# Map stage: inverse roots by Newton steps on VectorE, and a new order of feed-forward, squares and windows

## The reference

```python
x = x + conv_block(ln_c(x))      # windowed attention, then the map part
t = tokens(x)
t = t + ffn(ln_t(t))             # values rounded to fp8 (5,2) and fp16
x = from_tokens(t)

# map part of conv_block, on the attention result x2 (+ biases dw_b, fc2_b):
y   = gelu((layernorm(x2) * n2w + n2b) @ fc1_w + fc1_b)  # 96 -> 192
dw  = gelu(depthwise_conv_5x5(y) + dw_b)
x2  = (y + dw) @ fc2_w + fc2_b + x2                      # 192 -> 96

# ffn: h = relu(qlinear(t, W1, b1)), 96 -> 384; y = qlinear(h, W2, b2)
```

## Time and profile before

| | us |
|---|---|
| median of 3 runs | 7757.35 (7748.72 to 7774.06) |
| profiled execution | 7760.73, span 7758.4 |
| map stage in the profile | from about 3921 to the end |

### The profile page before, as it was taken

One profiled execution on the slowest core, in us unless ns is written; L12 is line 12 of the kernel. 1 busy time (PEld: TensorE's weight loads), 2 busy tenths in 40 slices (PEclk: granted clock), 3 DMA queues, 4 the chain that ended last, 5 costly groups with the idle time before them and its releaser, 6 DMA issues.

```text
span 7758.4 us, 207703 instructions
## 1 busy us (share of the span) xinstructions
PE 7010.4 (90%) x75964; PEld 4335.4 (56%) x75964; DVE 5160.8 (67%) x7973; ACT 4781.1 (62%) x7962; POOL 2218.8 (29%) x2024
## 2 busy tenths in 40 slices
PE   8969999999999999999958988989898889989987
PEld 3325555545545555555546666666666666666664
DVE  6867777777777777777745556556555655555564
ACT  6636656656655656566526666666666666666665
POOL 0013433334333443334312222222222222222221
PEclk9979999999999999999969999999999999999998
DMA  7744344444444444444323333333333333333332
GB/s 210 229 133 98 93 97 102 102 94 96 99 98 97 101 98 98 92 103 101 81 62 79 80 76 70 78 79 69 74 82 76 68 78 80 71 74 79 77 68 46
DMA packets 444703, 715.58 MB, mean 92 GB/s; under 512 B 116426, under 2 KB 358940, under 8 KB 419264
## 3 DMA queue, kind: packets, MB, share of 16 engines
q1 hardware_dynamic: 444209, 708.90, 38.8%
HBM read 395.33 MB, written 166.64 MB: 72 GB/s over the span
## 4 chain that ended last, share of the span: by engine, by line
SPq 19%; PE 19%; issue 4%; DVE 4%; ACT 2%; DMA 2%; DVEq 0%; ACTq 0%; POOLq 0%; POOL 0%
SPq L1101 19%; PE P L1269 6%; PE P L1258 3%; PE P L1328 3%; PE P L1247 3%; DVE Z L1685 2%; PE P L1278 2%; DMA YS<-Y 2%; PE P L1237 1%; DVE H L1714 1%; DVE H L1709 1%; ACT Y L1499 1%; PE P L1315 1%; ACT P L1505 1%; PE P L1213 0%
## 5 line engine op out<-in xcount | busy, mean ns | idle before, releaser
L820 DVE TENSOR_REDUCE NM<-P 128x4 f32<-128x1024 f32 x1444 | 1764.2, 1222 | 592.7 <-PE P L654 588.5
L768 ACT ACTIVATE PROB<-P 128x1024 f32<-128x1024 f32 x1444 | 1399.9, 1021 | 1025.8 <-PE P L669 1025.8
L1328 PE MATMUL P<-FC,XN 97*126 97x192 f32 x5408 | 1000.4, 330 | 41.1 <-ACT Y L1499 40.2
L1163 POOL TENSOR_TENSOR T<-T,Y 96x512 f16 (+1 forms) x260 | 305.9, 1176 | 2516.6 <-DVE Y L1718 2516.6
L1328 PEld LDWEIGHTS P<-FC,XN 97*126 97x126 f32 x5408 | 885.4, 188 | 196.1 <-issue 140.7
L669 PE MATMUL P<-QF,KS 32*128 32x256 f32 x11552 | 833.8, 403 | 112.0 <-DVE QF L815 111.3
L1499 ACT ACTIVATE Y<-P 126x384 f32<-126x384 f32 x1352 | 750.7, 618 | 238.2 <-PE P L1328 222.7
L669 PEld LDWEIGHTS P<-QF,KS 32*128 32x128 f32 x11552 | 525.0, 185 | 635.7 <-DVE QF L815 574.3
L505 POOL TENSOR_TENSOR Y<-XHS,RNS 96x512 f32<-96x512 f32 x304 | 598.0, 1993 | 820.3 <-DMA RNS<-rnorm 515.0
L677 PE MATMUL P<-PROB,V 128*32 128x256 f32 x11552 | 778.3, 387 | 1.4 <-ACT PROB L768 1.4
L1247 PEld LDWEIGHTS P<-Y,WC 127*50 127x50 f32 x19968 | 577.9, 140 | 180.1 <-DVE Z L1685 112.9
(11 more groups left out here) (149 smaller groups left out, 11273.6 us busy)
## 6 DMA issues: line engine op xcount, KB each, us to landing
YS<-Y SPq DMA_DIRECT2D x2080, 48.8 KB
RBC<-sums SPq DMA_DIRECT2D x456, 160.0 KB, 3.2
X<-x2map SPq DMA_DIRECT2D x52, 1344.0 KB, 8.3
XHS<-xhat SPq DMA_DIRECT2D x76, 768.0 KB, 6.3
RNS<-rnorm SPq DMA_DIRECT2D x38, 1536.0 KB, 9.5
x2map<-XHS SPq DMA_DIRECT2D x76, 768.0 KB
T<-in_x SPq DMA_DIRECT2D x52, 960.0 KB
out<-T SPq DMA_DIRECT2D x52, 960.0 KB, 4.9
```

Source lines behind the costliest of these rows:

```text
L768: A.activation(PROB[:, par, u:u + 2, :], P[:, B_ST[u]:B_ST[u] + 2, :], ACT.Exp, scale=DQ ** -0.5).then_inc(act_exp, 1)
L820: V_.tensor_reduce(NM[:, :, :].rearrange("p a (u d) -> p u a d", d=32)[:, 2 * i:2 * i + 2, :, DQ], P[:, B_S[0]:B_S[0] + 2, :].rearrange("p ...
L1328: m = M.matmul(P[0:KW, WBANK[r], i * MLP:(i + 1) * MLP], xnf[:, RI * WX * w:RI * WX * w + KW], FC1[:, :], start=True, stop=True)
```

## The change

- The root on ACT and the reciprocal on DVE are replaced: `parts` now adds 1e-5 to the variance (read from PSUM), makes a first guess by integer shift and subtraction, and refines it by three Newton steps of three DVE instructions each. `std2` and `std3` are gone. The gathered variance of `gather2` moves from bank 2 to the second half of bank 7; turn 1, which writes that bank, waits until DVE has read it.
- hidden 0 to 2 and output 0 (with hidden16, out16, hidden8 in their order on ACT and DVE) now run in the body of their own strip, among the last windows. On the other end, output 4 goes behind conv 11, and the DVE steps out16 3 and 4 go directly ahead of parts2. POOL's `end` 0 to 2 run at the end of their own strip's body, 3 and 4 in the next one, after means 0 and 1.
- The squares have five buffers instead of two (three of them lie in Z). The first five squares of strip u + 2 run at the end of body u, where PE also does var2 0 and 1; the rest follows in the next body.
- `begin` is cut into five pieces that follow means 2 to 6.
- Windows use banks 4 to 6 only; all of the orders of PE, ACT and DVE are rewritten. The SP queue issues the same transfers, with the condition on `begin` as a count of five.

```diff
-WBANK = [4 + r % 3 for r in range(12)] + [(0, 1, 4, 5, 6)[(r - 12) % 5] for r in range(12, NG)]
+NEARLY = 3
+WBANK = [4 + r % 3 for r in range(NG)]
...
-        B_VAR2, B_REP2, B_VAR3 = 7, 2, 7
+        B_VAR2, B_REP2, B_VAR3 = 7, 7, 7
...
+        SQB = [SQ[:, 0, :], SQ[:, 1, :]] + [zf[:, i * FT:(i + 1) * FT] for i in range(3)]
...
                 n = times(pool, u, NX)
...
-                    for j in range(NF):
+                    for j in range(NEARLY, NF):
                         end(o0, t0, j)
+                nxt = u + 1 if isinstance(u, int) else pool.snap(u + 1)
                 for j in range(NSLOT, NX):
                     means(n, third, j, first)
-                if follow:
-                    begin(u + 1 if isinstance(u, int) else pool.snap(u + 1))
+                    if follow:
+                        begin(nxt, j - NSLOT)
+                for j in range(NEARLY):
+                    end(times(pool, u, NF), third, j)
...
-                small(V.reciprocal(RCP[:, :], STD[:, :]))
+                V.tensor_scalar(STD[:, :], rep, 1e-5, None, ALU.add).then_inc(read, 1)
+                dve.wait_ge(read, nth)
+                small(V.tensor_scalar(bits, STD[:, :].bitcast(int32), 1, None, ALU.logical_shift_right))
+                small(V.tensor_scalar(bits, bits, -1.0, 1597463007.0, ALU.mult, ALU.add))
+                for _ in range(3):
+                    small(V.tensor_tensor(res, RCP[:, :], RCP[:, :], ALU.mult))
+                    small(V.scalar_tensor_tensor(res, res, -0.5, STD[:, :], ALU.mult, ALU.mult))
+                    small(V.scalar_tensor_tensor(RCP[:, :], res, 1.5, RCP[:, :], ALU.add, ALU.mult))
                 small(V.tensor_copy(RB[:, :], RCP[:, :]))
```

More of the change, by code:

```diff
@@ L1152, in _, with begin @@
             G = nc.gpsimd
[L1154 to L1159, removed]
+            def begin(u, j):
+                if j == 0:
+                    pool.wait_ge(xo_loaded, u * 32 + 32 if isinstance(u, int) else pool.snap(u * 32 + 32))
+                    pool.wait_ge(x2_loaded, u * 16 + 16 if isinstance(u, int) else pool.snap(u * 16 + 16))
+                t = T[:, tch(slot_of(pool, u), j)]
+                G.tensor_tensor(t, t, X2[:, 2 * W + j * FT:2 * W + (j + 1) * FT], ALU.add).then_inc(pool_x, 1)
             def end(o0, third, j):
@@ L1249, in conv, with turn @@
                 m.then_inc(pe_conv, 1)
-            def turn(n7, n12, j):
+            def turn(v, n7, n12, j):
                 if j == 0:
                     hold(pe, pe_passed, dve_ys, n12 + NCG)
+                if j == 1 and v is not None:
+                    hold(pe, pe_passed, dve_read2, v + 1)
                 if j >= 2:
@@ L1398, in body @@
                 beside(spread2, v, v7, 5)
-                turn(n7, n12, 6)
+                turn(v if follow else None, n7, n12, 6)
                 beside(spread2, v, v7, 6)
@@ L1452, in _ @@
             windows(0, 0, *range(NG))
+            for j in range(2):
+                var2(NL, j)
             strips(pe, body)
@@ L1455, in _ @@
             for j in range(NF):
-                hidden(last, j)
-                output(last, j)
+                if j >= 3:
+                    hidden(last, j)
+                if j >= 1:
+                    output(last, j)
         @block.scalar
@@ L1516, in turned, with body @@
                 z.then_inc(act_z, 1)
-            def body(u, prev, follow):
+            def body(u, prev, follow, more):
                 v = u + 1 if isinstance(u, int) else act.snap(u + 1)
@@ L1560, in body @@
                 convolved(n12, 11)
-                beside(std2, v)
+                ffn(out16, 4)
                 turned(n7, 0)
@@ L1598, in body @@
                 beside(windows, v26, 23)
+                hidden16(n5, 1)
                 beside(windows, v26, 24)
                 beside(windows, v26, 25)
+                ahead(square2, w, w7, 2)
+                ahead(square2, w, w7, 3)
+                out16(n5, 0)
+                hidden16(n5, 2)
+                ahead(square2, w, w7, 4)
+                out16(n5, 1)
             for j in range(NL):
                 square2(0, 0, j)
-            std2(0)
             windows(0, *range(NG))
+            for j in range(5):
+                square2(1, NL, j)
             strips(act, body)
@@ L1608, in _ @@
             for j in range(NF):
-                hidden16(last, j)
-                out16(last, j)
+                if j >= 3:
+                    hidden16(last, j)
+                if j >= 2:
+                    out16(last, j)
         @block.vector
@@ L1745, in body @@
                 add_centres(u, n12, 2)
-                ffn(out16, 2)
+                ffn(hidden8, 4)
                 add_centres(u, n12, 3)
@@ L1749, in body @@
                 add_centres(u, n12, 5)
-                dve.wait_ge(pool_x, u + 1)
-                ffn(hidden8, 4)
+                beside(sum2, v7)
                 add_centres(u, n12, 6)
-                beside(sum2, v7)
                 add_centres(u, n12, 7)
@@ L1787, in body @@
                 scale3(n5, 4)
+                hidden8(n5, 0)
+                hidden8(n5, 1)
+                out16(n5, 0)
+                hidden8(n5, 2)
+                hidden8(n5, 3)
+                out16(n5, 1)
+                out16(n5, 2)
             sum2(0)
-            dve.wait_ge(act_std, 1)
-            parts(1, dve_parts2)
+            parts2(0, 1)
             for j in range(NL):
@@ L1796, in _ @@
             for j in range(NF):
-                hidden8(last, j)
-                out16(last, j)
+                if j >= 4:
+                    hidden8(last, j)
+                if j >= 3:
+                    out16(last, j)
 def constants():
```

212 lines of the change are left out of this document (101 added, 111 removed).

## The result

The changed kernel takes 8036.32 us (median of 4 runs, 8032.76 to 8043.06) against 7759.12 us for the kernel before in the same comparison (4 runs, 7748.72 to 7774.06). The ratio is 1.0356, 95% interval 1.0343 to 1.0369: slower by 277 us, where about 193 were forecast. The direction was right; the time lies 86 us above the forecast of 7950 and 21 us above the range's upper end of 8015.

The account below looks back on a forecast made before the run. A 71.08 us ring, gone round 51 times, bounds the kernel; 41.2 + 12.8 + 20.9 = 74.9 us, so 7757.35 + 195 - 1.3, about 7950 us. Range 7730 to 8015 us; forecast's own 7880 to 8000.

Parts of the forecast that it names:

- The ring: Map stage: 51 equal strip-to-strip steps of 71.08 us set the time; forecast to become 74.9 us each.
- Part A: First windows matmul to first addition of centres, 40 sync-queue issues: 41.8 us before, forecast 41.2, moved feed-forward steps covered.
- Part B: Conv phase, first addition of centres to first turn: 13.66 or 12.55 us before, forecast 12.8 with low clock.
- Part C, the roots without POOL: Turns and fc2: twelve new DVE instructions make the roots 5.1 us instead of 2.4, hidden, leaving 15.85 us.
- rival 3: New DVE instructions take 0.45 us each, or feed-forward steps outlast the centres' landing: above 8015 us; chance 0.08.
- Part C, the port: Turns and fc2: POOL instructions hold up DVE's small ones beside parts2; PE stalls 2.8 to 4.0 us, taken as 3.4.
- Part C, the clock: Turns and fc2: after PE's stall, 1.2 GHz for some 3.3 us of dense work, costing 1.65 us.
- Outside the ring: First strip's roots +2.2 us; at the end parts3 +2.3, overlapped hidden/output rounds -5.3, last conv phase -0.5: together -1.3.
- Rival 1: Port costs little: parts2 ends by 7.1 us, stall 0 to 0.85 us, 7690 to 7737 us; chance 0.18.
- Rival 2: Port stalls PE but the clock stays up: ring 72.7 to 73.9 us, 7835 to 7900 us; chance 0.15.
- Rival 4: Reordering leaves the ring unchanged: the 40 issues dominate, other terms cancel, 7735 to 7780 us; chance 0.07.

Follow-up runs that it names:

- the two runs with old roots: Changed kernel with ACT's square root and DVE's reciprocal put back for both norms, 7873.9 us; put back for norm 2 alone, 7685.98 us.
- the kernel with POOL quiet: Changed kernel with POOL waiting for parts2 before means 2, end 3, 4 and begin moved behind means 3: 7690.17 us.
- both filled kernels: Unused matmuls between turn 3 and spread2 0: four in the changed kernel, 7929.86 us; two in the one with the residual add behind all copies, 7772.36 us.
- the old order with Newton roots: Kernel before with only the roots changed to Newton for both norms, old order, banks and buffers kept: 7790.18 us, ratio 1.0034.

## Why the prediction was right in direction and short in size

**The ring.** Right. All of the map stage is 51 equal steps, and (76.79 - 71.08) x 51 = +291 us of the spans' difference, 8036.0 - 7758.4 = 278.

**Part A,** forecast 41.2, measured 40.96: right. The cover held; no instruction of the feed-forward network moved into it came onto the ring. The statement beside it, that ACT is not on the ring at the table loads, so that their loss gains nothing, is true of the old order only. In the new one, with three banks, the loads of norm 3's root would cost about (7874 - 7686) / 51 = 3.7 us a ring, by the two runs with old roots. Norm 3's Newton root was needed for the new order; I priced the parts of the change one by one and missed that two of them hold each other up.

**Part B,** forecast 12.8, measured 12.95: right, with the low clock before conv 3 as said. It is low for 3.4 us in one kind of strip and for 6.8 us in the other, and slows fewer chunks in the first.

**Part C, the roots without POOL,** forecast 5.1 us and no wait: measured 5.1 us, right to the tenth. The 0.45 us apiece of rival 3 is out.

**Part C, the port,** the mechanism as in the earlier trace rows: right, by the rows above and by the kernel with POOL quiet. The size fell short at one choice. parts2 was to end 9.1 us after the first turn, or 10.3 if the copies block too; it ended at 10.4, and the wait was 4.0 us, the upper bound. I had taken 3.4, the middle. Two copies block, 0.6 us each. The Trainium skill, "GPSIMD Engine Reference", section 8 (Key points), which excepts no GpSimd instruction, would have given the 4.0; the trace agrees with it here. Term: +0.6 us a ring, +31 us.

**Part C, the clock.** This step failed, in size: 1.65 us was forecast, with bounds of 1.2 and 2.1. Measured, 22.87 - 15.81 - 4.0 = 3.1 us are lost beyond the wait on average. The clock itself is 2.1 and 2.8 us of that in the two kinds of strip (22.50 and 23.23 against 20.40 with the wait filled), 2.5 on average. The rest is 0.6 us that I left out: spread2 stands 4.2 us later than in the quiet kernel and not 4.0, and 0.4 us stay in both filled kernels, whose cause was not tried. The clock was sized too low because from the earlier trace rows I took 3.3 us of dense work. That low stretch is 3.4 us long in all, and PE idles in its first 0.8 us. Here the stretch is 6.8 us, with 5.1 or 6.6 us of work in it. The trace of the kernel before has stretches of 6.8 us as well, but only four beside 73 of 3.4 in the map stage. What makes one long or short stays open. Term: 3.1 instead of 1.65, +1.4 us a ring, +74 us.

The two terms together: 0.6 + 1.4 = 2.0 us, against 76.79 - 74.9 = 1.9 measured. The port's term stayed within its bounds, the clock's did not, and the latter alone put the time outside the range: with 3.4 and 3.1 us the sum gives 8025 us, with 4.0 and 2.1 it gives 8004. There is a slip in the forecast's own range, too: its upper ring of 75.9 us leaves out the 0.4 us of doubt on A and B, and should be 76.35 (8025 us). Even so the measured 76.79 lies above it.

**Outside the ring,** forecast -1.3 us; the spans give 278 - 291 = -13. The time to the first landing is 5.1 us less (the earlier trace rows against 4036.99) where 2.2 more was forecast. But the kernels here that share this stage have it anywhere from 4024 to 4041, so I don't read a cause from it. After the last landing it is 82.9 us instead of 91.1, 8.2 less where 3.5 was forecast. Which of its three terms is larger wasn't tried.

**The rivals.** Rival 1, the port costing little, at 7690 to 7737 us: ruled out for the changed kernel, but it is what the kernel becomes when POOL is kept away (7690, the range's lower end). Its point of decision, parts2 ending by 7.5 us after the turn, was placed rightly: the kernels of the new order with 4.0, 5.3 and 5.9 us are faster, those with 8.3 and 10.4 slower. (With both old roots it is 4.0 and the kernel still slower, by part A.) Rival 2, the clock staying up, at 7835 to 7900: ruled out by the stretches; the kernel with the long wait filled, which has this case made by hand, took 7930. Rival 3, slow new instructions: the measured 8036 lies where it was put, above 8015, but its mechanism is out, as they take 0.22 to 0.29 us alone. Rival 4, an unchanged ring: out, as it grew by 5.7 us.

## What to carry to other kernels

A chain of small dependent VectorE instructions with inputs in SBUF should have GpSimd idle beside it: count the GpSimd instructions that its neighbours release, and charge the chain with each one's length, less that of the instruction it holds up (here 5.0 us for six that last 6.5). Price a wait of TensorE on the critical ring as the wait plus up to half of the work that falls into the low-clock stretch after it, and allow for the longest such stretch in the trace, not the commonest. When a change removes an operation and takes away the slack that hid it (here, as argued, two of five banks), price the one with the other, as undoing one part alone can cost more than it gives.

## What the runs showed of the hardware

- A VectorE instruction of 0.22 to 0.29 us became 0.8 to 1.3 us beside one GpSimd instruction and ended up to 0.15 us after it; adds of 96 partitions did this, and so did a copy of one partition by 400 values.
- After TensorE's idle stretch of 4.0 us the granted clock was at 0.50 for 6.8 us in all 50 strips. After one of 1.9 us it was so for 6.8 us in 43 strips of 50, for 3.4 us in five, and not at all in two. With the shorter wait 3.4 us at the low clock cost 1.7 us of the turn phase and 6.8 us cost 3.1 to 3.3. With the longer one the 6.8 us cost 2.1 or 2.8. After the 0.63-us wait of the old order with Newton roots the clock did not fall.
- Unused matmuls in such a wait gave the clock's loss back: 8036 to 7930, 7937 to 7772 and 7690 to 7634 us. Where they outlasted the wait (10.54 us in one of 3.6) they cost time, 7690 to 7948 us.
- A table load on ScalarE took 1.28 us with no idle time between it and its function (5043.91 + 1.28 = 5045.19, the root at 5045.21).
- Integer instructions on VectorE (shift, and multiply-add on 96x128 int32) took 0.22 us, no more than a cast.
